# A four-block attention and gate layer on one core: one weight half is prepared earlier, half of a weight merge is moved into the first step, and the first normalisation is shared by two engines

## The reference

```python
xn = layernorm(x)                       # over the 1024 features
q, k, v = xn @ Wq.T, xn @ Wk.T, xn @ Wv.T     # 32 query heads, 8 key/value heads, 128 wide
q, k = rmsnorm(q, q_norm_w), rmsnorm(k, k_norm_w)
attn = softmax(q @ k.T / sqrt(128) + alibi_bias)  # causal
s = (attn @ v) @ Wo.T
g = silu(xn @ W.T + bias + lora_out)    # lora_out: sum over 8 adapters of rank 16
out = x + s * g
```

## Time and profile before

| | us |
|---|---|
| median of 3 runs | 2688.27 (2685.08 to 2691.18) |
| profiled execution: device time | 2691.18 |
| profiled execution: span of the core | 2689.4 |
| TensorE busy | 2591.1 (96%) |
| ScalarE busy | 1771.1 (66%) |
| GpSimd busy | 1705.5 (63%) |
| VectorE busy | 1648.2 (61%) |

### The profile page before, as it was taken

How to read it: one execution, slowest core, us unless ns; L and a number is a source line. 1 busy time by engine, 2 the same in 40 slices (tenths; PEclk the granted TensorE clock), 3 DMA queues, 4 the chain that set the end, 5 groups by cost and what they waited for, 6 DMA issues and landing times.

```text
span 2689.4 us, 39881 instructions
## 1 busy us (share of the span) xinstructions
PE 2591.1 (96%) x13840; PEld 2297.7 (85%) x13840; DVE 1648.2 (61%) x3530; ACT 1771.1 (66%) x4635; POOL 1705.5 (63%) x835
## 2 busy tenths in 40 slices
PE   5689999999999999999999999999999999999997
PEld 4578888888888888888888888888888888888886
DVE  6446566657667556566566666556666755655666
ACT  4366666666776667667767667666767666666763
POOL 3377877876667656656667656565666756655653
PEclk9899999999999999999999999999999999999999
DMA  7888788775445333433335433433334533333323
GB/s 259 269 269 281 240 266 263 256 259 190 128 145 174 109 119 100 154 111 104 110 106 183 133 117 104 154 105 106 112 108 136 180 110 106 118 110 118 111 69 129
DMA packets 179192, 418.45 MB, mean 156 GB/s; under 512 B 31152, under 2 KB 72240, under 8 KB 178096
## 3 DMA queue, kind: packets, MB, share of 16 engines
q1 hardware_dynamic: 177728, 414.78, 47.4%
q10 hardware_dynamic: 1264, 1.12, 0.1%
HBM read 343.48 MB, written 89.13 MB: 161 GB/s over the span
## 4 chain that ended last, share of the span: by engine, by line
PE 89%; DVE 3%; ACT 2%; DMA 2%; POOL 1%; issue 1%; SPq 1%; POOLq 0%; DVEq 0%; ACTq 0%
PE proj L486 21%; PE proj L488 21%; PE proj L487 21%; PE tr L581 5%; PE sc L486 3%; PE sc L487 3%; PE sc L488 3%; PE ot L487 3%; PE tr L561 3%; PE ot L488 3%; PE ot L486 3%; PE tr L554 1%; DMA wu<-xtok 1%; SPq L313 1%; DVE acc L1226 1%
## 5 line engine op out<-in xcount | busy, mean ns | idle before, releaser
L985 POOL TENSOR_TENSOR wl<-wl,wh 128x896 fp32r<-128x896 f32 x436 | 948.9, 2206 | 608.7 <-ACT wh L740 608.6
L486 PE MATMUL proj<-wh,xh 128*128 128x448 f32 x1792 | 673.8, 376 | 25.0 <-POOL wl L985 17.5
L487 PE MATMUL proj<-wl,xh 128*128 128x448 f32 x1792 | 661.1, 369 | 0.0
L488 PE MATMUL proj<-wh,xl 128*128 128x448 f32 x1792 | 661.1, 369 | 0.0
L996 POOL TENSOR_TENSOR wb_lo<-wb_lo,wb_hi 128x1024 fp32r<-128x1024 f32 x128 | 307.2, 2400 | 315.6 <-ACT wb_hi L750 315.6
L807 ACT ACTIVATE misc<-misc,negmax 128x128 f32<-128x128 f32 (+3 forms) x512 | 286.8, 565 | 250.2 <-DVE negmax L1202 250.2
L486 PE MATMUL proj<-o_hi,wb_hi 128*128 128x512 f32 x1024 | 424.9, 415 | 9.3 <-issue 6.1
L1226 DVE TENSOR_TENSOR acc<-acc,proj 128x512 f32<-128x512 f32 x480 | 327.7, 684 | 156.6 <-PE proj L488 155.3
L786 ACT ACTIVATE pT_hi<-tr 128x512 fp32r<-128x512 f32 (+3 forms) x512 | 197.3, 440 | 334.5 <-PE tr L581 334.5
L740 ACT ACTIVATE wh<-wl 128x896 fp32r<-128x896 f32 x436 | 395.5, 966 | 33.0 <-DMA wl<-wu 32.5
L488 PE MATMUL proj<-o_hi,wb_lo 128*128 128x512 f32 x1024 | 404.6, 395 | 0.0
(11 more groups left out here) (125 smaller groups left out, 4366.6 us busy)
## 6 DMA issues: line engine op xcount, KB each, us to landing
wl<-wu SPq DMA_DIRECT2D x436, 448.0 KB, 3.9
wb_lo<-wo_in SPq DMA_DIRECT2D x128, 512.0 KB, 3.3
wu<-xtok SPq DMA_DIRECT2D x13, 1792.0 KB, 10.2
wo_in<-wo SPq DMA_DIRECT2D x32, 512.0 KB, 6.0
xtok<-wa SPq DMA_DIRECT2D x52, 256.0 KB, 4.6
wu<-xtok SPq DMA_DIRECT2D x13, 896.0 KB, 5.6
gate_dram<-misc SPq DMA_DIRECT2D x32, 256.0 KB, 5.1
xtok<-xT SPq DMA_DIRECT2D x28, 256.0 KB, 5.1
```

Source lines behind the costliest of these rows:

```text
L486: pe.matmul(out, hi_l, hi_r, start=first, stop=False, skip_group_check=onto)
L487: pe.matmul(out, hi_l, lo_r, start=False, stop=False, skip_group_check=onto)
L488: return pe.matmul(out, lo_l, hi_r, start=False, stop=last, skip_group_check=onto)
L985: pool.tensor_tensor(w_slot(wl, w), w_slot(wl, w, True), w_slot(wh, w), ALU.subtract).then_inc(w_ready, 1)
```

## The change

Seven edits, all of them in the part of the program that ends with step (0, 3):

- VectorE scales tiles 2 and 3 of the first tokens; ScalarE scales only 0 and 1. GpSimd and TensorE wait for the new semaphore `x_scaled` where they read those tiles.
- The high and low parts of the first adapter matrix lie in `pT_hi` and `pT_lo` instead of `qT_hi` and `qT_lo`, so that they last until step (0, 0).
- Group 1's places are exchanged: half 0 in `xtok`, half 1 in `acc`. SP loads half 0 as soon as the tokens are transposed, ahead of group 0's sums, and loads half 1 when `acc` is free. It doesn't load the gate's second rows there.
- VectorE makes the four subtractions of group 1's half 0 between the pieces of P6, P7 and P4 of group 0, where it merged the gate before.
- The gate's half 1 is loaded after group 1's half 0 is stored, is merged in step (0, 0) behind the pieces of P1 and P2 and ahead of the transposed probabilities (TensorE and VectorE), and is stored behind the loads of P6 and P7.
- ScalarE splits P2 of group 1 in step (0, 0) behind `normalise` instead of ahead of the first exponentials.
- GpSimd in steps (0, 1) and (0, 3) makes the low parts of the products first and the subtractions of group 2 behind them.

```diff
@@ prep_place
-            return flat(acc if (g, h) in ((0, 0), (1, 0)) else xtok)
+            return flat(acc if (g, h) in ((0, 0), (1, 1)) else xtok)
@@ SP
             store_halves(0, 1)
+            sp.wait_ge(weff_out[0], 16 * NK)
             sp.wait_ge(tr_done, TR["x", 0, 2 * NP - 1] + 1)
-            load_gate_rows(1)
+            load_weights(1, 0)
+            load_gate_weights(1, 0)
             store_sums(0, 0)
             store_sums(0, 1)
-            store_gate_rows(1)
-            sp.wait_ge(weff_out[0], 16 * NK)
+            store_halves(1, 0)
             sp.wait_ge(prep_tst[0], 16)
             sp.wait_ge(w_ready, 2 * P5 + 1 - ON_DVE)
...
             load_weights(1, 1)
             load_gate_weights(1, 1)
+            load_product(0, P3)
...
             store_halves(1, 1)
+            copy_b(0)
             load_w(HW + 1)
+            store_sums(1, 0)
             load_product(1, P2)
-            store_sums(1, 0)
+            sp.wait_ge(prep_tst[0], 32)
+            load_gate_rows(1)
@@ SP, step
                     load_product(n + 1, P7)
+                    if n == 0:
+                        store_gate_rows(1)
+                        sp.wait_ge(weff_out[1], 16 * NK)
                     if new is not None:
                         sp.wait_ge(prep_tst[1], 16 * new)
                         load_weights(new, 0)
@@ PE, step
+                if m == 0:
+                    pe.wait_ge(scored, NT)
+                    for k in range(NK):
+                        merge_gate(1, k)
+                    pe.wait_ge(weff_ready, 2 * NK)
@@ ACT
-            ln_scale(0, 2)
-            ln_scale(0, 3)
...
-            split_product(1, P2)
...
                 normalise(m)
+                if m == 0:
+                    split_product(1, P2)
@@ GpSimd, step
-                if j in (1, 3) and n + 2 < HKV:
+                if j in (1, 3) and n > 0 and n + 2 < HKV:
                     weight_sums(n + 2, j // 2)
...
+                if j in (1, 3) and n == 0:
+                    weight_sums(2, j // 2)
@@ DVE
             ln_factors(0)
+            dve.wait_ge(ln_newton, 5)
+            for t in (2, 3):
+                dve.tensor_scalar(xtok[:, t, :], xtok[:, t, :], rinv_x[:, t:t + 1], shift_x[:, t:t + 1],
+                                  ALU.mult, ALU.add).then_inc(x_scaled, 1)
...
-            for i, (p, t) in enumerate(((P6, 0), (P6, 1), (P7, 0), (P7, 1))):
-                take_piece(0, p, t)
-                merge_gate(1, 2 * i)
-                merge_gate(1, 2 * i + 1)
+            take_piece(0, P6, 0)
+            take_piece(0, P6, 1)
+            weight_sum(1, 0, P5)
+            take_piece(0, P7, 0)
+            weight_sum(1, 0, P7)
+            take_piece(0, P7, 1)
+            weight_sum(1, 0, P6)
             take_piece(0, P4, 0)
+            weight_sum(1, 0, P4)
             take_piece(0, P4, 1)
...
                 if n == 0 and j == 0:
-                    weight_sums(1, 0)
+                    weight_sums(1, 1)
```

More of the change, by code:

```diff
@@ L64, in ln_group, with scaled_rows @@
     return 6 if b == 1 else 5
+def scaled_rows(b, tiles):
+    return min(tiles, 2) if b == 0 else 4 * b - 2 + tiles
 def unit_pieces(n, j):
@@ L201, in build_layer @@
             sem(n) for n in ("u_dve", "scored", "rs_ready", "prob_ready", "tr_free", "ot_free", "out_free"))
-        w_first = sem("w_first")
+        w_first, x_scaled = sem("w_first"), sem("x_scaled")
         newton, k_ready, q_ready = sem("newton"), sem("k_ready"), sem("q_ready")
@@ L242, in build_layer @@
         lora_a_raw, lora_b_raw = misc[:, 0:TILE], misc[:, TILE:2 * TILE]
-        lora_a_hi, lora_a_lo = flat(qT_hi), flat(qT_lo)
+        lora_a_hi, lora_a_lo = pT_hi[:, 0:TILE], pT_lo[:, 0:TILE]
         lora_b_hi, lora_b_lo = wb_hi[:, 1, :], wb_lo[:, 1, :]
@@ L384, in _ @@
             store_halves(0, 1)
+            sp.wait_ge(weff_out[0], 16 * NK)
             sp.wait_ge(tr_done, TR["x", 0, 2 * NP - 1] + 1)
-            load_gate_rows(1)
+            load_weights(1, 0)
+            load_gate_weights(1, 0)
             store_sums(0, 0)
             store_sums(0, 1)
-            store_gate_rows(1)
-            sp.wait_ge(weff_out[0], 16 * NK)
+            store_halves(1, 0)
             sp.wait_ge(prep_tst[0], 16)
             sp.wait_ge(w_ready, 2 * P5 + 1 - ON_DVE)
[L393 to L401, removed]
             load_weights(1, 1)
             load_gate_weights(1, 1)
+            load_product(0, P3)
+            sp.wait_ge(prep_tst[1], 16)
+            sp.dma_start(rel_sb[:], rel).then_inc(rel_in, 16)
             load_w(HW)
             store_halves(1, 1)
+            copy_b(0)
             load_w(HW + 1)
+            store_sums(1, 0)
             load_product(1, P2)
-            store_sums(1, 0)
+            sp.wait_ge(prep_tst[0], 32)
+            load_gate_rows(1)
             def load_x(b):
@@ L548, in turn_x @@
                 else:
-                    pe.wait_ge(ln_ready, 4 * b + (4 if p == P4 else 2))
+                    if b == 0 and p == P4:
+                        pe.wait_ge(x_scaled, 2)
+                    pe.wait_ge(ln_ready, scaled_rows(b, 4 if p == P4 else 2))
                 bank = turn_bank(key)
@@ L640, in _ @@
                 turn_x(("x", 0, f))
-            for i, (p, t) in enumerate(((P6, 0), (P6, 1), (P7, 0), (P7, 1))):
-                piece(0, p, t)
-                merge_gate(1, 2 * i)
-                merge_gate(1, 2 * i + 1)
-            for p in (P4, P5, P3):
+            for p in (P6, P7, P4, P5, P3):
                 for t in range(2):
@@ L650, in _ @@
                     turn_queries(0, 0)
-            pe.wait_ge(weff_ready, 2 * NK)
             def step(n, j):
@@ L1015, in x_sum @@
                 if what == P7:
-                    pool.wait_ge(ln_ready, 4 * b + 4)
+                    pool.wait_ge(ln_ready, scaled_rows(b, 4))
+                    if b == 0:
+                        pool.wait_ge(x_scaled, 2)
                     pool.tensor_tensor(r21, r11, r21, ALU.subtract).then_inc(sum_ready, 1)
@@ L1221, in add_out @@
                 if (v, c) == (0, 0):
-                    dve.wait_ge(prep_tst[0], 32)
+                    dve.wait_ge(prep_tst[1], 32)
                 if v % 32 < 2:
```

2 lines of the change are left out of this document (removed).

## The result

| | median us | runs | ratio to before, 95% interval |
|---|---|---|---|
| before | 2688.05 | 20 | |
| after | 2696.99 | 20 | 1.0031 [1.0024, 1.0038] |
| forecast | 2684.8 (2673 to 2694) | | |

The changed kernel is slower by 0.31%: 8.3 us by the ratio, 8.9 us between the two medians, where 3.5 us less was forecast. One launch of the kernel before took 14591 us; all the others lie between 2684 and 2694 us, and it hardly moves the median. The profiled execution of the changed kernel took 2700.03 us over a span of 2698.2 us, 8.8 us more than the span of before.

The account below looks back on a forecast made before the run. After 187.3 us TensorE is busy 2466.7 of 2502.1 us; before that, its waits come from SP's one queue of loads and stores. Gain 19.2 us at head 1, 3.5 left at head 5: 2688.27 - 3.5 = 2684.8 us, range 2673 to 2694.

Parts of the forecast that it names:

- part 4 of the prediction: Heads 1 to 5: late gate store, group 2 loads and sums give back the gain, from 19.2 us to 3.5.
- everything behind head 5: From head 5 on both programs do the same, so the gain of 3.5 us stays to the end.
- Opening: Up to head 0: tokens transposed at 52.3 us instead of 54.30, P4 starting at 74.7 and ending 2.7 us later.
- The forecast's 89.6 us for P3's low part: Ahead of head 1: P3's load issued at 81.6, landed after 3.9, split about 1 us, low parts 2.1 us each.
- Head 1: First score maximum of head 1 at 120.6 us instead of 139.84, a gain of 19.2 us; the moved merge ends at 116.1.
- Head 2: Gate's second half lands at about 123, then group 2's first weights load; head 2 at 142.2, a gain of 16.7 us.
- the landing of the sum: Half 1 of group 1, stored at 104, lands by 114; P6 is there at 118, so the landing is just hidden.
- Heads 3 and 5: GpSimd's later subtractions delay group 2's sum stores: gain 13.3 us at head 3, less 2 for the clock, then 3.5 at head 5.
- rival 2: SP's order in steps (0, 1) to (1, 0): stores landing in 9.9 instead of 5.9 us, slower, 2692.8 or 2695; chance 0.15.
- The pause's price: TensorE restarts at the low clock after idling: 2 us off the gain at head 3, 1.2 more by head 5.

Follow-up runs that it names:

- The last experiment: Changed kernel with GpSimd's old order, P7's pieces first, keys scaled early in seven steps, plus gate stores ahead of P6 and P7 loads on SP: 2669.47 us, ratio 0.9928.
- The early keys: Keys scaled right behind the row factors in seven steps: 2681.09 us in the kernel before; 2671.97 against 2680.4 us in the changed kernel with old order and P7's pieces first.

## Why the prediction was wrong

The mechanism was on paper; several of its terms were too small, and one was put at nothing. The step that failed most is the landing of the gate's second half (part 4 of the prediction), and the one put at nothing is everything behind head 5.

1. *Opening.* Right within the spread. The tokens were transposed by 49.40 us (52.3 forecast), group 1's tiles landed at 71.2 (73), P4 started at 72.87 (74.7), and head 0 came 6.8 us early (4.9; 4.3 to 5.5 in the three other versions with this opening). The forecast's 89.6 us for P3's low part does not follow from its terms (81.6 + 3.9 + 1.0 + 2.1 is 88.6 for the first tile); GpSimd had both tiles done at 87.65. The idle of TensorE in front of P4 was 9.3 us.
2. *Head 1.* 17.2 us of the 19.2. The merge ended 2.4 us later than laid out.
3. *Head 2, the step that failed most.* I wrote: "The gate's second half is stored behind the merge and lands at about 123." It landed at 129.2. I had placed the landing of the sum ahead of it and called it hidden, since P6 came in time; but the same landing held SP's queue, and the gate's stores stand in that queue. Without that wait the stores could have followed the merges to about 119.5 and landed 3.6 us later, as they did, at 123. The last experiment shows this for the queue: with the stores ahead, they end at 118.1 instead of 122.1. Between heads 1 and 2, 7.1 us were lost where 2.5 were forecast. In the final time, exchanging the order brought 2.5 us and not 4.6, since P6 then came late.
4. *Heads 3 and 5.* Given back 4.9 and 8.6 us, where 3.4 and 9.8 were forecast. The store of half 1's sums went out at 214.30. The landings of the two stores took 6.9 and 6.8 us, not 5.9 and not the 9.9 of rival 2. The pause's price was there too: behind 5.15 us of waiting at 142.52 and 7.05 us at 175.58 TensorE was granted 0.50 of its clock, which is 1.2 GHz. After, the windows behind the two pauses, columns as in the earlier trace rows:

```profile
142.50:146.50 4.00, 3.04 (x10) 2.22 (x10) 1.75 (x3) 0.27 (x1) 1.20 (x1) 0.50 1.00 339
...
175.50:179.50 4.00, 3.92 (x12) 3.72 (x13) 2.79 (x7) 1.70 (x6) 3.75 (x2) 0.50 1.05 289
```

   The forecasts that "ScalarE should wait for P6's load in step (1, 0)" (4.86 us at 222.24) and that the subtractions end some 8 us behind the low parts came out.
5. *Behind head 5.* I wrote that from there "the two programs do the same", and of everything after 187.3 us that nothing in the change touches it, though GpSimd's new order in step (0, 3) lies there. They do the same instructions, but a late store is handed on: 3.4 us more at head 7, from loads queued behind the late ones. The version with the old order in (0, 3) alone shows it: from head 6 to head 7 it takes 17.3 us again. And instructions alike in both kernels met at the port in one and not in the other: the changed kernel lost about 2 us each at heads 11 and 19, and was spared about 2 us at head 7. The early keys brought nearly the same in both kernels, so no part of the 8.3 us is shown to come from the port.
6. *The rivals.* Rival 2 named the right sign, the right queue and the point of decision: 19 us given back between heads 1 and 5; it was 20.6. Its price stood on the wrong term (landings of 9.9 us). At 0.15 it was too cheap: all three stores sit in one queue, and each of the forecast's times in it was a least time.

The misses from head 1 on, in us: 2.0 at head 1, 4.6 to head 2, 1.5 to head 3, -1.2 to head 5, 3.4 to head 7, 2.0 from there to the end, together 12.3, which is the distance from a gain of 3.5 to a loss of 8.8. They are read from one trace of each kernel, with the spread told above.

## What to carry to other kernels

Follow a queue by its waits and not by the need of the data: a landing that comes in time for its reader can still hold the issue behind it. Where a step of preparation is made late, look two steps on, at what is loaded into the place that it frees. Before "the rest is the same" is written, look for pairs of VectorE and GpSimd instructions that start within a tenth of a microsecond of each other: any shift, also a gain, decides them anew. Here an order that keeps them apart in seven steps was worth 7.8 us, more than twice the gain that the change was forecast to bring.

## What the runs showed of the hardware

- VectorE instructions with two inputs in SBUF stood still beside GpSimd's: 0.17 to 2.06 us for eight columns, 0.68 to 2.64 us for a scaling of 128x512.
- A few hundredths of a microsecond decide who gets the port: GpSimd's recorded start was 0.02 us ahead at 340.04 and 501.53, and VectorE went first; it was 0.04 us ahead at 257.54, 345.38 and 508.75 and 0.05 at 419.02, and VectorE waited.
- The issue of one store of 256 KB to `weff` took SP 0.42 to 2.58 us in the changed kernel (median 0.77; the one of 2.58 at 120.65, when all merges were done) and 0.36 to 0.87 us in the last experiment (median 0.84). Eight loads of group 2, four of 256 KB and four of 128 KB, took 3.96 us, about 0.5 each. What makes the stores differ was not tried.
- A store of 1792 KB landed after 12.0 us at 104.25 and after 6.9 and 6.8 us at 164.05 and 214.30.
